# A two-block convolution kernel: programs written out by images, the first unit's planes formed on GpSimd, and the scale applied with the high and low parts

## The chip, the cores and the metric

The kernel runs on one core of a Trainium2 chip. The metric is the device time of one execution in microseconds. Engine names in the profile: PE is TensorE, DVE VectorE, ACT ScalarE, POOL GpSimd, SP SyncE.

## The reference

The input x is 4 images of 96 channels and 128 x 128 pixels, float32. Two residual blocks follow, each on a group normalisation (32 groups of 3 channels, no learned factors):

```
x = x + attention(gn(x))
x = x + conv_block(gn(x))

attention: layer norm over channels -> 1x1 convolutions to q (96), k (24), v (24)
           -> depthwise 3x3 -> attention over channels, 8 heads of 12 x 12,
              with l2-normed q and k and a temperature -> 1x1 projection
conv_block(y): cat(conv1x1(y), conv3x3(y), conv5x5(y), conv3x3 dilated by 2 (y)) -> 1x1 to 96
```

All four convolutions of the second block and the 1x1 behind them are linear, so the kernel folds them into one 5x5 convolution.

## The kernel before, in words

An image stays in SBUF as X (96 partitions x 16384). Per image there are these stages.

1. Projection (PE L712, in 32 tiles of 4 rows): ScalarE norms a tile (L915), PE projects it, ScalarE squares (L921), VectorE sums and scales (L1237, L1252), GpSimd adds a bias and stores it in another order (L596).
2. Depthwise 3x3 (PE L733 to L735, 24 chunks): VectorE builds band matrices (L1278), ScalarE evicts chunks (L947, L950) and sums the next image's rows.
3. Gram products of q and k (PE L761) on strips that VectorE copies (L1303), then a softmax chain of small steps, then attention (PE L796). VectorE adds the residual, which gives x1 in X, 2 x 512 columns at a time (L1364, 16 per image), and ScalarE sums squares of x1 (L1021). A group is averaged by a small product (`group_mean`, L693). Columns of `small` hold the statistics: MG the group mean, VG its variance, SA the scale, SBI the bias.
4. The 5x5 convolution, in 11 units of 12 rows (4 blocks of 3 rows; the last has fewer). It is a fast convolution: from normed rows (`y2`) differences in the row direction give five planes per block (`pln`, `planes`, L1408 to L1424), sums of neighbouring columns give `cs`, both are split into a high f16 part (`hi`, copied to `hi2`; ACT `highs`, L1052 to L1063) and a low one (`low`; DVE `lows`, L1474). DMAs place the low parts on other partitions beside the high ones (`place_first`, `place_groups`, `place_low`, SP and ACT queues), and PE multiplies with the weights in five groups (L865; L860 are products with low parts put off to the end of a group). VectorE combines the products (L1505, L1523), forms output rows (L1536), GpSimd adds the residual (L611) and SP writes out. For units 2 to 10 GpSimd makes two of the planes (L621).

Unit 0 has five blocks, the first being the rows at the image's edge, and goes in two parts: planes 3 and 4 first (part 0), planes 0 to 2 then (part 1), so that PE can begin early. Its first 7 rows are normed by ScalarE (L1039), the rest by VectorE (L1560).

Each engine runs a program of its own, and the order is written out by hand. Each of the five programs has an outer loop over the 4 images (`Fori(0, B)`), with counters in semaphores. While PE would idle between statistics, `keep_warm` (L688) gives it products of no use.

In the set-up, VectorE makes 32 bn_stats over image 0's rows (L1162) as they land, between steps on the weights. PE folds the convolutions to `folded` (L675), ScalarE copies them (L894). `split_weights` on GpSimd (L544 to L589) scales them by WSC, makes the fast convolution's weights and splits them into `wh` and `wl`; it runs in image 0, beside the depthwise stage. PE waits for its end (`s_split`) before the first group mean of the Gram stage, VectorE before the first column sums of unit 0.

## Time and profile before

| | us |
|---|---|
| median of 3 runs | 1769.56 |
| lowest and highest | 1764.85, 1773.46 |
| the profiled execution | 1766.19 |
| its span, first to last instruction | 1764.4 |

The profiled execution is one run; its span leaves out what lies before the first and after the last instruction. The mean granted clock of TensorE is 0.969 of full speed (2.4 GHz); the lower level, 1.2 GHz, reads 0.50 in a window. A line of the timeline gives start, duration, engine, source line, operation, output<-inputs, shapes, the count of like instructions merged, and in brackets the idle time before and what ended it.

### The profile page before, as it was taken

The page shows a single profiled execution, that of the slowest core. Times are in us where ns is not written, and L with a number is a line of the kernel's source. Part 1 is how long each engine was busy: PE and PEld are TensorE (multiplying, and loading weights), DVE is VectorE, ACT ScalarE, POOL GpSimd, SP SyncE. Part 2 cuts the span into 40 slices and gives each one's busy share as a digit, 9 for nine tenths or more (in the row PEclk, how much of TensorE's full clock was granted, in tenths as well). Part 3 has the DMA queues.
Part 4 walks back from the last instruction along what each step waited for, and adds up shares of the span by engine and source line. Part 5 has one row for each costly group of instructions (what it writes and reads, how often), then busy time and mean ns, then how long its engine had stood idle before and what let it go on. Part 6 is the DMA issues. An engine that isn't in the chain of part 4 may idle for free.

```text
span 1764.4 us, 40341 instructions
## 1 busy us (share of the span) xinstructions
PE 1674.1 (95%) x13429; PEld 1578.1 (89%) x13429; DVE 1502.6 (85%) x1950; ACT 1012.0 (57%) x1638; POOL 541.0 (31%) x351
## 2 busy tenths in 40 slices
PE   5989988999999999899999999999999999989998
PEld 5989857999989996899999997799999999689998
DVE  5788848999868877999978886899997887699996
ACT  2746656564366667656438566755636666664551
POOL 5799910223254000122328000032235500012222
PEclk9999978999999997999999999799999999899999
DMA  7012113566611210566650220266661021055453
GB/s 186 0 32 67 46 31 79 152 166 170 167 46 32 72 40 1 127 176 163 171 142 0 67 71 6 54 156 167 171 176 56 27 71 46 1 121 142 123 151 98
DMA packets 101196, 166.24 MB, mean 94 GB/s; under 512 B 40010, under 2 KB 74411, under 8 KB 100940
## 3 DMA queue, kind: packets, MB, share of 16 engines
q1 hardware_dynamic: 77932, 138.95, 31.1%
q10 hardware_dynamic: 23168, 26.04, 4.6%
q8 instruction: 55, 0.90, 0.2%
q14 instruction: 41, 0.34, 0.1%
HBM read 52.20 MB, written 25.17 MB: 44 GB/s over the span
## 4 chain that ended last, share of the span: by engine, by line
PE 50%; issue 17%; DVE 17%; POOL 9%; DMA 2%; ACT 2%; SPq 2%; DVEq 1%; POOLq 0%; ACTq 0%
PE ps L865 14%; PE ps L712 12%; PE ps L733 6%; PE ps L735 5%; PE ps L734 5%; PE ps L761 3%; PE ps L796 3%; DVE region L1474 3%; DVE region L1408 2%; DVE region L1505 2%; POOL region L611 2%; DVE region L1523 2%; POOL W L552 1%; POOL W L571 1%; DVE region L1536 1%
## 5 line engine op out<-in xcount | busy, mean ns | idle before, releaser
L865 PE MATMUL ps<-region,W 128*96 128x256 f16 (+4 forms) x7156 | 803.3, 272 | 15.6 <-DMA region<-region 15.6
L865 PEld LDWEIGHTS ps<-region,W 128*96 128x96 f16 (+2 forms) x7156 | 780.6, 122 | 31.4 <-issue 22.0
L621 POOL TENSOR_TENSOR region<-region 96x528 f32<-96x528 f32 (+1 forms) x72 | 96.4, 1343 | 924.9 <-DVE region L1474 923.6
L1278 DVE TENSOR_TENSOR region<-V,band 128x2322 f32<-128x2322 f32 (+2 forms) x104 | 260.8, 2518 | 59.9 <-PE ps L735 57.6
L1058 ACT ACTIVATE region<-region 96x1584 f16<-96x1584 f32 (+2 forms) x88 | 110.8, 1301 | 331.2 <-DVE region L1419 317.9
L733 PE MATMUL ps<-region 128*128 (+1 forms) x1152 | 229.1, 281 | 12.6 <-DVE region L1278 9.2
L735 PE MATMUL ps<-region 128*128 (+1 forms) x1152 | 223.7, 276 | 0.0
L734 PE MATMUL ps<-region 128*128 (+1 forms) x1152 | 223.4, 276 | 0.0
L712 PE MATMUL ps<-proj,region 96*128 96x240 f32 x1024 | 210.7, 369 | 8.3 <-DVE region L1536 8.3
L712 PEld LDWEIGHTS ps<-proj,region 96*128 96x128 f32 x1024 | 196.1, 192 | 22.0 <-issue 8.7
L1505 DVE SCALAR_TENSOR_TENSOR region<-ps,small,region 96x768 f32<-96x768 f32 (+1 forms) x220 | 203.7, 989 | 12.6 <-PE ps L865 11.3
L1474 DVE TENSOR_TENSOR region<-region 96x792 f16<-96x792 f32 (+10 forms) x176 | 197.5, 1180 | 5.0 <-ACT region L1058 4.8
L611 POOL TENSOR_TENSOR region<-region,X 96x1536 f32<-96x1536 f32 (+1 forms) x44 | 124.0, 2818 | 224.7 <-DVE region L1536 224.7
L733 PEld LDWEIGHTS ps<-region 128*128 128x128 f32 x1152 | 175.7, 193 | 17.9 <-issue 15.7
L596 POOL TENSOR_TENSOR region<-region,cbias 128x576 f32 (+1 forms) x124 | 175.8, 1418 | 46.7 <-DVE region L1252 43.2
L734 PEld LDWEIGHTS ps<-region 128*128 128x128 f32 x1152 | 176.0, 193 | 0.0
L735 PEld LDWEIGHTS ps<-region 128*128 128x128 f32 x1152 | 175.9, 193 | 0.0
L950 ACT ACTIVATE region<-ps 128x768 f32 (+1 forms) x80 | 65.8, 822 | 144.2 <-PE ps L735 144.2
L1052 ACT ACTIVATE region<-region 96x1584 f16<-96x1584 f16 (+2 forms) x88 | 113.9, 1295 | 0.3
L1252 DVE TENSOR_TENSOR region<-ps,region 128x576 f32<-128x576 f32 x124 | 94.0, 758 | 18.4 <-DVE region L1242 5.4
L915 ACT ACTIVATE region<-X,small 96x512 f32 (+1 forms) x128 | 101.6, 802 | 8.2 <-issue 7.4
L1536 DVE TENSOR_TENSOR region<-region 96x256 f32<-96x256 f32 (+3 forms) x176 | 88.4, 543 | 20.1 <-DMA out_dram<-region 18.4
(196 smaller groups left out, 2075.5 us busy)
## 6 DMA issues: line engine op xcount, KB each, us to landing
region<-region SPq DMA_DIRECT2D x116, 247.5 KB, 4.0
region<-in_x_dram SPq DMA_DIRECT2D x128, 192.0 KB, 2.4
out_dram<-region SPq DMA_DIRECT2D x40, 576.0 KB, 4.2
region<-region ACTq DMA_DIRECT2D x72, 247.5 KB, 2.5
X<-in_x_dram SPq DMA_DIRECT2D x30, 576.0 KB, 6.0
region<-region SPq DMA_DIRECT2D x36, 247.4 KB, 4.9
X<-in_x_dram SPq DMA_DIRECT2D x19, 384.0 KB, 11.3
region<-region SPq DMA_DIRECT2D x24, 185.6 KB, 3.5
```

The lines of the kernel that those rows point to most:

```text
L596: pool.tensor_tensor(Q[:, :, bass.ds(t * AR, AR)].rearrange("p c r -> p r c"), pq[:, i], cbias[:].unsqueeze(1).broadcast_to([P, AR, CO]), ...
L611: pool.tensor_tensor(ob[:, 0:r * W], ob[:, 0:r * W], X[:, bass.ds(u * UR * W, r * W)], ALU.add).then_inc(s_res, 1)
L712: last = mm(ps[:, 2 * i + r // 2, r % 2 * 256:r % 2 * 256 + NP], y1[:, i, r * W:(r + 1) * W], proj[:], start=True, stop=True)
L733: mm(o, T[:, i, 3 * c + 1, 0:W], src, start=True, stop=False)
L734: mm(o[:, 1:H], T[:, i, 3 * c, 0:W], src[:, 0:H - 1], start=False, stop=False)
L735: last = mm(o[:, 0:H - 1], T[:, i, 3 * c + 2, 0:W], src[:, 1:H], start=False, stop=True)
L865: last = mm(o, w, src, start=k == 0, stop=k == len(steps) - 1, skip_group_check=split and ck > 0)
L1052: act.activation(hi2[0:C, a:e, x:z], hi[0:C, a:e, x:z], ACT.Copy).then_inc(s_h, 1)
L1058: act.activation(dst[0:C, a:e, x:z], src, ACT.Copy).then_inc(s_h, 1)
L1278: v.tensor_tensor(T[:, i, 3 * c:3 * c + m].rearrange("p m (i j) -> p m i j", j=3), taps.broadcast_to([P, m, BW // 3, 3]), mask.broadcast_t ...
L1474: v.tensor_tensor(low[:, :, x:end], src, hi[0:C, a:e, x:end], ALU.subtract).then_inc(s_l, 1)
L1505: step = lambda dst, g, factor, src: v.scalar_tensor_tensor(row(dst), product(i, g, blocks), col(factor), row(src), ALU.mult, ALU.add).the ...
```

## The change

PE's and VectorE's loops over the images become Python loops, so that their programs hold four copies of an image's instructions, with waits on constants; the other three engines keep theirs. The scaling of the folded weights goes from GpSimd to ScalarE, behind the projection of image 0. PE no longer waits for `s_split` before the Gram stage. Six bn_stats go ahead of VectorE's wait for the weights. Unit 0's planes and wide column sums come from GpSimd, on x1 itself, and begin when two of x1's tiles are added: no scale is in them, and since they are differences the mean falls out, except for plane 4, to which VectorE adds the mean's share later, and the first block, which VectorE fills with x1 less the mean. `highs` and `lows` of unit 0 multiply by SA. Unit 0's buffers move. ScalarE's order in unit 0 puts the high part of part 1 before the copy of part 0; the first set's squares are taken in two halves; 22 warm-up products replace 40. VectorE's wait for `s_split` moves to the first low parts.

```diff
-        LOWF_AT, PLNF_AT, Y2F_AT = LOW_AT, Y2_AT - 5 * PLAIN, ACC_AT
-        YF = 5 * OR + 2
-        assert LOWF_AT + 5 * BLK // 2 <= PLNF_AT and Y2F_AT + YF * RW <= OB_AT + UR * W
+
+
+        LOWF_AT, PLNF_AT, CSF_AT, Y2F_AT = LOW_AT, Y2_AT - 5 * PLAIN, RING // 2 + 5 * BLK // 2, RING + 5 * BLK // 2
+        YF = OR + 2
+        assert LOWF_AT + 5 * BLK // 2 <= PLNF_AT and 5 * NPT * PC <= 5 * BLK // 2 and (YF + 5) * RW <= 5 * BLK // 2
...
-        N_SPLIT = 13 + NRT * 6 + 2
+        N_SPLIT = 12 + NRT * 6 + 2
...
-                pool.wait_ge(s_fold, N_COPIES + 5)
-                pool.wait_ge(s_dv, N_WSC)
-                plain = W32[:, FOLDED_AT:FOLDED_AT + 5 * 5 * C]
-                step(pool.tensor_scalar(plain, plain, col(WSC), None, ALU.mult))
+                pool.wait_ge(s_fold, N_COPIES + 6 + 5)
...
+                def first_planes():
+
+                    _, _, pln, yb, cs = buffers(0)
+                    rows = X[:, 0:(4 * OR + OR) * W].rearrange("p (r j c) -> p r c j", j=HC, c=2)
+                    taps = lambda t, c, count: rows[:, t + 1:t + 1 + 4 * OR, c] \
+                        .rearrange("p (k t) j -> p k t j", t=OR)[:, :, 0:count]
+                    slots = lambda x, end, c: pln[:, 1:5, x * RW:end * RW] \
+                        .rearrange("p k (t c j) -> p k t c j", c=2, j=PC)[:, :, :, c, 1:1 + HC]
+                    plane = lambda k, end, x: pln[:, k:end, x * RW:(x + 1) * RW]
+                    twice = f32at(Y2F_AT + YF * RW, 5 * RW).rearrange("p (k e) -> p k e", k=5)
+
+                    def done(n):
+                        pool.wait_ge(s_fp, b * NFP + n + START)
+
+                    def column_sums(k, end, x, y):
+                        pairs = pln[:, k:end, x * RW:y * RW].rearrange("p k (q e) -> p k q e", e=RW)
+                        dst = cs[0][:, k:end, 0:PC] if x == 3 else cs[1][:, k:end]
+                        pool.tensor_tensor(dst.rearrange("p k (q j) -> p k q j", j=PC), pairs[:, :, :, PC:RW],
+                                           pairs[:, :, :, 1:1 + PC], ALU.add).then_inc(s_fp, 1)
+
+                    def take(dst, a, d):
+                        pool.tensor_tensor(dst, a, d, ALU.subtract).then_inc(s_fp, 1)
+
+                    def point_0_and_inf(k, end, n):
+                        done(n)
+                        take(twice[:, k:end], plane(k, end, 1), plane(k, end, 0))
+                        take(plane(k, end, 2), plane(k, end, 2), plane(k, end, 1))
+                        done(n + 2)
+                        take(plane(k, end, 0), twice[:, k:end], plane(k, end, 0))
+                        take(plane(k, end, 2), plane(k, end, 2), plane(k, end, 1))
+                        done(n + 4)
+                    pool.wait_ge(s_x1, b * SETS * 2 + 2 + START)
+                    pool.wait_ge(s_o, (b * SETS + 2) * AR + START)
+                    for c in range(2):
+                        take(slots(3, 5, c), taps(2, c, 2), taps(1, c, 2))
+                    pool.memset(pln.rearrange("p k (q j) -> p (k q) j", j=PC)[:, :, 0:PC:PC - 1], 0.0).then_inc(s_fp, 1)
+                    pool.memset(yb, 0.0).then_inc(s_fp, 1)
+                    done(3)
+                    take(twice[:, 1:5], plane(1, 5, 4), plane(1, 5, 3))
+                    done(5)
+                    take(plane(1, 5, 3), twice[:, 1:5], plane(1, 5, 3))
+                    for n in (8, 10):
+                        for c in range(2):
+                            take(slots(4, 5, c)[:, :, 0], slots(4, 5, c)[:, :, 0], taps(1, c, 1)[:, :, 0])
+                        done(n)
+                    column_sums(1, 5, 3, 4)
+                    for c in range(2):
+                        take(slots(0, 3, c), taps(2, c, 3), taps(0, c, 3))
+                    point_0_and_inf(1, 5, 13)
+                    column_sums(1, 5, 0, 3)
+                    pool.wait_ge(s_pl0, b * NPL0 + 1 + START)
+                    own = yb.rearrange("p r e -> p (r e)")
+                    take(pln[:, 0, 0:3 * RW], own[:, 2 * RW:], own[:, 0:3 * RW])
+                    point_0_and_inf(0, 1, 19)
+                    column_sums(0, 1, 0, 3)
...
+                first_planes()
...
-            with pe.Fori(0, B) as b:
+            for b in range(B):
...
-                pe.wait_ge(s_split, N_SPLIT)
...
                 group_mean(st, VG, sv + N_VG2, 7)
-                keep_warm(0, 40)
+                keep_warm(0, 22)
...
-                                pe.wait_ge(s_h, n * NH + 4 + START)
+                                pe.wait_ge(s_h, n * NH + 5 + START)
...
+                with act.If(b < 1):
+                    act.wait_ge(s_dv, N_WSC)
+                    for k in range(5):
+                        act.activation(folded[:, k], folded[:, k], ACT.Copy, scale=col(WSC)).then_inc(s_fold, 1)
...
+                def squared_halves(k, n):
+
+                    for half in range(2):
+                        act.wait_ge(s_x1, (b * SETS + k) * 2 + half + 1 + START)
+                        squared(k, half, 2, n + half)
+                squared_halves(0, 0)
+                with act.Fori(1, SETS - 1) as k:
                     act.wait_ge(s_x1, (b * SETS + k + 1) * 2 + START)
-                    squared(k, 0, 1, k)
-                for half in range(2):
-                    act.wait_ge(s_x1, (b * SETS + SETS - 1) * 2 + half + 1 + START)
-                    squared(SETS - 1, half, 2, SETS - 1 + half)
+                    squared(k, 0, 1, k + 1)
+                squared_halves(SETS - 1, SETS)
...
-                        act.activation(dst[0:C, a:e, z:end], src, ACT.Copy).then_inc(s_h, 1)
+                        act.activation(dst[0:C, a:e, z:end], src, ACT.Copy, scale=1.0 if whole else col(SA)).then_inc(s_h, 1)
                     if whole == 0:
-                        for part in range(2):
-                            act.wait_ge(s_pl, n * NPL + (3, 7)[part] + START)
-                            plain(hi, part)
-                            act.wait_ge(s_pl, n * NPL + (4, 8)[part] + START)
-                            sums(hi, part)
-                            copied(part, 4 * part + 2)
-                            if part == 0:
-                                midway()
+                        act.wait_ge(s_pl0, b * NPL0 + 4 + START)
+                        plain(hi, 0)
+                        act.wait_ge(s_pl0, b * NPL0 + 6 + START)
+                        act.wait_ge(s_fp, b * NFP + 11 + START)
+                        sums(hi, 0)
+                        act.wait_ge(s_fp, b * NFP + 23 + START)
+                        plain(hi, 1)
+                        copied(0, 2)
+                        act.wait_ge(s_fp, b * NFP + 24 + START)
+                        sums(hi, 1)
+                        midway()
+                        copied(1, 6)
                     else:
-                        act.wait_ge(s_pl, n * NPL + 6 + START)
...
-                rows_normed(0, 0)
                 highs(0, 0, 0, lambda: rows_normed(1, 1))
...
+            statistics(0, 3)
             dve.wait_ge(s_w, NLOADS * 16)
...
-            statistics(0, 6)
+            statistics(3, 6)
...
-            with dve.Fori(0, B) as b:
+            for b in range(B):
...
-                yf, yn = buffers(0)[3], buffers(1)[3]
-                v.memset(yf[:, 0:2], 0.0)
-                for y in (yf[:, 2:], yn):
-                    v.memset(y.rearrange("p r (c j) -> p (r c) j", c=2)[:, :, 0:PC:PC - 1], 0.0)
+                _, _, pln0, yb, cs0 = buffers(0)
+                plane0 = lambda k, x, end: pln0[:, k, x * RW:end * RW]
+
+                def first_done(k):
+                    dve.wait_ge(s_pl0, b * NPL0 + k + START)
+
+                def first_block_rows():
+
+                    dve.wait_ge(s_fp, b * NFP + 4 + START)
+                    v.tensor_scalar(yb.rearrange("p r (c j) -> p r c j", c=2)[:, 2:, :, 1:1 + HC],
+                                    X[:, 0:OR * W].rearrange("p (r j c) -> p r c j", j=HC, c=2),
+                                    col(MG), None, ALU.subtract).then_inc(s_pl0, 1)
+                    first_done(1)
+                    own = yb.rearrange("p r e -> p (r e)")
+                    v.tensor_tensor(plane0(0, 3, 5), own[:, 2 * RW:4 * RW], own[:, RW:3 * RW], ALU.subtract).then_inc(s_pl0, 1)
+
+                def first_part():
+
+                    first_done(2)
+                    v.scalar_tensor_tensor(plane0(0, 3, 4), plane0(0, 3, 4), -2.0, plane0(0, 4, 5),
+                                           ALU.mult, ALU.add).then_inc(s_pl0, 1)
+
+                    dve.wait_ge(s_fp, b * NFP + 10 + START)
+                    one = pln0[:, 1:5, 4 * RW:5 * RW].rearrange("p k (c j) -> p k c j", c=2)[:, :, :, 1:1 + HC]
+                    v.tensor_scalar(one, one, col(MG), col(MG), ALU.add, ALU.add).then_inc(s_pl0, 1)
+
+                def first_sums():
+
+                    first_done(4)
+                    v.tensor_tensor(cs0[0][:, 0, 0:PC], plane0(0, 3, 4)[:, PC:RW], plane0(0, 3, 4)[:, 1:1 + PC],
+                                    ALU.add).then_inc(s_pl0, 1)
+                    one = pln0[:, :, 4 * RW:5 * RW]
+                    v.tensor_tensor(cs0[0][:, :, PC:2 * PC], one[:, :, PC:RW], one[:, :, 1:1 + PC], ALU.add).then_inc(s_pl0, 1)
+                yn = buffers(1)[3]
                 v.memset(col(MG), 0.0)
                 dve.wait_ge(s_x1, (b + 1) * 2 * SETS + START)
                 moments(st, tsums[:, 0:2 * SETS], MEAN2, MEAN)
                 assert st.n == N_MEAN2
+                v.memset(yn.rearrange("p r (c j) -> p (r c) j", c=2)[:, :, 0:PC:PC - 1], 0.0)
                 dve.wait_ge(s_pst, pst + 6 + START)
                 link(st, v.tensor_copy(col(MG), ps[0:C, 7, 0:1]))
                 link(st, v.tensor_tensor(col(DEV), col(MEAN2), col(MG), ALU.subtract))
                 link(st, v.tensor_tensor(col(VAR), col(SHIFT), col(SHIFT), ALU.mult))
                 link(st, v.scalar_tensor_tensor(col(VAR), col(DEV), col(DEV), col(VAR), ALU.mult, ALU.subtract))
-                dve.wait_ge(s_xs, (b + 1) * (SETS + 1) + START)
-                link(st, v.tensor_reduce(col(SQ), tsums[:, AT:], AX.X, ALU.add))
+                first_block_rows()
+                dve.wait_ge(s_xs, (b + 1) * (SETS + 2) + START)
+                link(st, v.tensor_reduce(col(SQ), tsums[:, 2 * SETS:], AX.X, ALU.add))
                 link(st, v.scalar_tensor_tensor(col(VG), col(SQ), 1.0 / (H * W), col(VAR), ALU.mult, ALU.add))
                 assert st.n == N_VG2
+                first_part()
                 dve.wait_ge(s_sqrt, b * 3 + 4 + START)
                 link(st, v.reciprocal(col(SA), col(RSTD)))
                 st.done(v.scalar_tensor_tensor(col(SBI), col(MG), -1.0, col(SA), ALU.mult, ALU.mult))
                 assert st.n == N_AFF2
+                first_sums()
...
+                        if whole == 0:
+                            v.scalar_tensor_tensor(low[:, :, x:end], src, col(SA), hi[0:C, a:e, x:end],
+                                                   ALU.mult, ALU.subtract).then_inc(s_l, 1)
+                            return
...
-                FIRST_ACT = 7
                 dve.wait_ge(s_st, sv + N_AFF2 + START)
-                v.tensor_scalar(yf[:, 2 + FIRST_ACT:].rearrange("p r (c j) -> p r c j", c=2)[:, :, :, 1:1 + HC],
-                                X[:, FIRST_ACT * W:(UR + OR) * W].rearrange("p (r j c) -> p r c j", j=HC, c=2),
-                                col(SA), col(SBI), ALU.mult, ALU.add).then_inc(s_y2v, 1)
-                planes(0, 0)
+                dve.wait_ge(s_split, N_SPLIT)
+                for part in range(2):
+                    lows(0, 0, 0, 0, part)
                 planes(1, 1)
                 lows(1, 1, 0, 1)
                 first_rows(0, 0, BPU)
```

## Rows read from the trace of the kernel before

**Rows 1.** The page: busy us of each engine, share of the span, instructions

```profile
PE 1674.1 (95%) x13429; PEld 1578.1 (89%) x13429; DVE 1502.6 (85%) x1950; ACT 1012.0 (57%) x1638; POOL 541.0 (31%) x351
```

**Rows 2.** The page: the chain that ended last, shares by engine

```profile
PE 50%; issue 17%; DVE 17%; POOL 9%; DMA 2%; ACT 2%; SPq 2%; DVEq 1%; POOLq 0%; ACTq 0%
```

**Rows 3.** Set-up: timeline of DVE and PE; landing of the first three row loads

```profile
31.37 10.77 DVE L1162 BATCH_NORM_STATS2 region<-X 96x6 f32<-96x512 f32 x18
...
39.20 0.48 PE L682 MATMUL ps<-small,region 96*96 96x5 f32 x2 [1.20 <-ACT region L895]
...
DMA to landing us min/median/max: 5.2/6.2/7.2
```

**Rows 4.** Depthwise stage of image 0: timeline, and a window (seventh value: granted clock)

```profile
105.98 8.36 POOL L544 TENSOR_SCALAR W<-W,small 96x2400 f32<-96x2400 f32 x1 [0.48 <-POOL region L596]
...
116.35 0.79 PE L733 MATMUL ps<-region 128*128 x2 [5.64 <-DVE region L1278]
...
114.00:122.00 8.00, 5.65 (x26) 5.66 (x27) 5.67 (x3) 0.00 (x0) 7.56 (x7) 0.59 0.09 25
```

**Rows 5.** Timeline of PE: start of the Gram products in images 0 and 1

```profile
226.48 0.48 PE L693 MATMUL ps<-small,gmean 96*96 96x1 f32 x2 [8.53 <-POOL W L589]
226.82 9.04 PE L761 MATMUL ps<-region 128*120 128x240 f16 x64
...
653.13 6.75 PE L761 MATMUL ps<-region 128*120 128x240 f16 x64
```

**Rows 6.** Timeline at the first, third (PE) and second (DVE) border between images

```profile
496.52 0.67 PE L712 MATMUL ps<-proj,region 96*128 96x240 f32 x2 [3.26 <-DVE region L1536]
...
1338.89 1.48 PE L712 MATMUL ps<-proj,region 96*128 96x240 f32 x6 [2.32 <-DVE region L1536]
...
920.13 0.15 DVE L1255 COPY small<-small 96x1 f32<-96x1 f32 x1 [1.97 <-issue]
```

**Rows 7.** Timeline of image 1 from the x1 tiles to unit 1

```profile
676.49 1.22 DVE L1364 SCALAR_TENSOR_TENSOR X<-ps,X 96x1024 f32 x1
...
692.51 0.08 DVE L1364 DVE_READ_ACCUMULATOR X<-ps,X  x1
...
697.08 1.21 ACT L1039 ACTIVATE region<-X,small 96x896 f32<-96x896 f32 x1 [0.42 <-DVE small L1387]
...
701.52 1.31 ACT L1058 ACTIVATE region<-region 96x1320 f16<-96x1320 f32 x1 [3.23 <-DVE region L1419]
...
705.18 0.65 SPq L365 DMA_DIRECT2D region<-region  x1
...
708.48 2.85 PE L865 MATMUL ps<-region,W 128*96 128x256 f16 x24 [1.69 <-DMA region<-region]
708.95 1.86 ACT L1058 ACTIVATE region<-region 96x1980 f16<-96x1980 f32 x1 [1.54 <-DVE region L1415]
...
714.36 1.25 DVE L1411 TENSOR_TENSOR region<-region 96x1056 f32<-96x1056 f32 x1 [0.19 <-DVE region L1474]
...
717.16 0.90 ACT L1098 ACTIVATE region<-ps,small 96x768 f32<-96x768 f32 x1 [2.62 <-PE ps L865]
...
719.84 2.51 ACT L1058 ACTIVATE region<-region 96x1584 f16<-96x1584 f32 x2 [1.78 <-DVE region L1415]
...
735.21 0.64 PE L860 MATMUL ps<-region,W 96*96 96x256 f16 x4 [1.29 <-DMA region<-region]
```

**Rows 8.** Timeline: DVE beside POOL, with one operand from PSUM and with none

```profile
215.03 0.59 POOL L568 TENSOR_TENSOR W<-W 96x192 f32<-96x192 f32 x1
215.04 0.59 DVE L1211 SCALAR_TENSOR_TENSOR small<-small 96x1 f32<-96x1 f32 x1
...
877.48 4.71 DVE L1505 SCALAR_TENSOR_TENSOR region<-ps,small,region 96x768 f32<-96x768 f32 x5
877.53 2.90 POOL L611 TENSOR_TENSOR region<-region,X 96x1536 f32<-96x1536 f32 x1 [14.67 <-DVE region L1536]
```

**Rows 9.** Groups of POOL by form, whole span (count, busy us, mean ns, idle before)

```profile
L621 POOL TENSOR_TENSOR region<-region 96x528 f32<-96x528 f32 x64 | 83.8, 1311 | 923.6 <-DVE region L1474 923.6
```

105 lines of the change are left out of this document (41 added, 64 removed).

## The prediction

> **What bounds the kernel now.** I read four views in this order: the busy shares, the chain of waits, the timeline around the places that the diff touches, and the windows with the granted clock. TensorE is busy 95% of the span and VectorE 85% [rows 1], and half of the chain that ended last is PE work [rows 2]. So a change pays only where PE stands still or runs slowly. The edited places that show this are four: the set-up; the first image's depthwise stage and the wait behind it; the three borders between images; and, four times, the passage from the last x1 tile to the second unit of the 5x5 stage.
>
> **The change part by part.** Gains are negative.
>
> *a. Set-up.* Six of the 24 statistics that VectorE makes before the weight maximum move ahead of the wait for the weights. Eighteen take 10.77 us, so six take 3.6 [rows 3]. The three loads that they read land 5.2 to 7.2 us after issues from 7.1 to 8.1, that is by 15.3, and VectorE would otherwise wait, so they fit before its set-up steps. But VectorE then comes to the maximum 3.6 us earlier, at about 38.5, and the product that it reads starts at 39.20 [rows 3]. It waits to about 39.8, which leaves some 2.2 of the 3.6. Ends: 0 (the steps behind are held) and -3.6. I take **-2.2**.
>
> *b. Depthwise stage of image 0.* GpSimd's scaling of the folded weights (L544) lasts 8.36 us; beside it VectorE's band matrix waits, and PE idles 5.64 us [rows 4]. The change gives that scaling to ScalarE as five instructions on 480 elements, at a time when ScalarE has finished its tiles and the first eviction is still ahead: nothing on the path. GpSimd's other splitting steps move up by as much and now meet the early bands, for which I keep 0.8 of the wait. After the gap the granted clock is 0.59 over 8 us, the lower level for most of it, which is 3.3 us of lost PE time [rows 4]. Sum -(5.64-0.8)-3.3 = **-8.1**. Ends: -4 (the splitting steps take the gap's place) and -9.
>
> *c. The wait for the split weights.* In image 0 PE stands 8.53 us in front of the group mean until GpSimd's last memset. Then its first 64 Gram products take 9.04 us, where image 1 takes 6.75: the clock again [rows 5]. The wait is deleted, and the rest (strips, sums) was there. VectorE and PE now do the strips and small statistics beside GpSimd's last steps; I put 1 us against it. -8.53-2.29+1.0 = **-9.8**. Ends: -6 and -10.8. What is late next is the weights' placing on SP, which follows the split; it moves up by b's 7 us or so and the first unit comes over 40 us later, so nothing waits.
>
> *d. Borders between images.* The PE and VectorE programs are written out, so their jump back is gone. PE's gap there is 3.26 us at the first border, 2.32 at the third, the second between them, together 8.2 [rows 6]. The row names VectorE's last outputs, but only PE's second tile needs what came last; VectorE itself idles 1.97 us after it with "issue" as the cause [rows 6], and both then start together: it is the jump. GpSimd, ScalarE and SP keep their loops, whose jumps lie in idle time. I take **-7.6**, keeping 0.2 per border. Ends: 0 (the new code is fetched just as late) and -8.2. The Trainium skill, Advanced Engine Details and Errata, Control Flow Timing, gives about 108 ns for a compare-and-branch; by that page's figure, an estimate, the three borders would give 0.3 us and the forecast would be 1737.
>
> *e. From x1 to the second unit, four times.* Times of image 1 [rows 7]. The scale is known at 697.08 (call it T). Then rows are scaled, planes formed, and only at 701.52 is the first high part made; the first low part is sent at 705.18, PE starts at 708.48, VectorE starts unit 1's planes at 714.36, ScalarE its high parts at 719.84, and PE gets the low parts that unit 1 needs at 735.21. With the change the planes exist at T. ScalarE's own work between 701.52 and 719.84 is the 18.3 us less its idle times of 1.54 and 1.78, and less some 0.4 of the 2.62 in which its queue issued three DMAs: 14.6 us. That chain now starts at T, if nothing else is late: unit 1's high parts start at T+14.7 instead of T+22.8, a gain of 8.
>
> T itself moves, and this is where I choose. GpSimd makes 24 instructions per image. From a two-input row of 192 elements (0.59 us) and one of 528 (1.311) [rows 8, 9] comes 0.18 us + 2.15 ns per element. Up to the wide column sums these are two of 512, six of 528, four of 256, one of 264, two of 768, one of 792 and two memsets: 2.6+7.9+2.9+0.8+3.7+1.9+0.8 = 20.6 us. They start when two tiles of x1 are added, at 676.5 [rows 7], so they end near 697.5. VectorE's statistics run from 692.6 to T [rows 7], so they meet GpSimd's last four or five. [Rows 8] show what that costs: a two-input VectorE instruction on a single column (L1211) took 0.59 us, starting and ending with GpSimd's L568. So each such step waits out the GpSimd instruction in flight, and they alternate. Placing the three two-input steps of the variance, the two of the first block's rows, the one of VG, and the one of SBI in this way, against GpSimd's 528, 528, 792, 396 and four of 132, T comes at about 702, 5 us later. Uncontended it would be 697. ScalarE's chain adds 0.3 for the first column sums. So unit 1's high parts start at 702+14.9 = 716.9, 2.9 us earlier. PE starts unit 0 at about 709 (low part sent at T+3.7, the same 3.3 to land), 0.5 later than now, but its second half (93 products at 0.11) finds its parts there. Everything behind 719.84 follows at the same distances, and PE, which would come to the low parts at 730.6, waits to 732.3. Gain 2.9 x 4 = **-11.6**. Ends per image: -7 (T stays; GpSimd's last planes still hold the copies by 1.3) and +2 (T at 707). The 18 fewer warm-up products leave PE idle for some 3 us before unit 0; if that lost the clock as b's gap did, 3.3 us would go, of which 1.7 lie in the wait before 732.3. That is inside the ends.
>
> The Trainium skill, SBUF — State Buffer, SBUF: two separate sides, says that a VectorE instruction in a two-port mode also takes the shared ports, with one input too. No row here shows it for one input. By the page the two added tensor_scalars would each wait out one more short GpSimd step, an estimated 1 us per image, and the forecast would be 1734.
>
> GpSimd's work during the adding of x1 costs VectorE nothing: those adds have one operand in PSUM, and the like instruction L1505 ran 4.71 us for five beside L611's 2.90, both their usual lengths [rows 8]. Register sums saved by constant waits, the moved memsets and the halved first square (0.3 us) I cost at nothing: they lie in the slack above.
>
> **Sum.** -2.2-8.1-9.8-7.6-11.6 = -39.3. The profiled execution took 1766.19 us around a span of 1764.4, so 1726.9 there. The median of the three runs is 1769.56, 3.4 above it; the forecast is for the median, 1730.
>
> **The rivals.** *No collision in the statistics (T stays).* For it: the steps are short and the order of GpSimd's list might just miss them. Against: L1211. Then e gives 7 x 4 = 28: 1714. *Only image 0 gains.* T moves to 705 or later and eats the rest of e, and the borders stay: a, b, c alone, -20: 1750. For it: the alternation could be worse than I placed it. *The x1 adds are blocked* (the one on the slower side). If each of GpSimd's instructions held up a VectorE add of x1, as L568 held L1211, the stage, which PE and VectorE share with no slack, would stretch by up to GpSimd's 20.6 us per image, 82 in all, without e's gain: 1769.6-27.7+82 = 1824. It decides against the change from about 7 us per image on. Against it: L1505 beside L611. *The written-out programs are read late*, at borders and elsewhere, and take back what the rest gives: within 0.5% of 1769.6. Against it: image 0, whose code also comes for the first time, shows no such gaps in its 5x5 stage. That PE's deleted wait is implied by another would be seen as the gap staying; the group mean's inputs are ready before, so I give it no chance of its own.
>
> **How the numbers follow.** Forecast case 0.62, no collision 0.15, image 0 alone 0.13, code read late 0.05, x1 blocked 0.05. A measurement here can tell 0.5%, 8.8 us. The first three are faster (0.90), the fourth the same (0.05), the last slower (0.05). The unknown costs move the likeliest case from 1714 to 1748; the range takes in both neighbours, 1710 to 1752, and leaves out the last two and some edges.
>
> **What would show it.** In image 0: no gap of PE before L733 around 110, none before the group mean, the Gram products near 6.75 us. At the borders: PE gaps under 0.5 us. In each image: two-input statistics steps of VectorE longer than 0.3 us beside GpSimd, T 4 to 6 us later, and 14 to 15 us from T to unit 1's high parts. Wrong would be: x1 adds (1.22 us now) longer, borders with 2 us or more, or T unmoved.

## The result and the profile after

The changed kernel takes 1724.91 us (median; 1724.12 to 1725.26), the kernel before 1768.41 in the same comparison: a ratio of 0.9751, 95% interval 0.9726 to 0.9776. That is 43.5 us less; the forecast was 39.3 less and 1730, so the time lies in the range. The profiled execution took 1725.26 around a span of 1723.0, 41.4 under the span before. The lines move: PE's projection is now L772, the depthwise products L793 to L795, the Gram products L821, the group mean L753, the keep-warm products L748, attention L855, the 5x5 products L924 and L919; VectorE's band matrices are L1346, its x1 additions L1432, unit 0's low parts L1554; ScalarE's high parts L1122; GpSimd's first planes L632.

The page of the changed kernel, parts 3 (the instruction queues: packets, MB, share of the DMA engines) and 4 (the chain, shares by engine):

```profile
q8 instruction: 47, 0.77, 0.2%
q14 instruction: 34, 0.28, 0.1%
...
PE 70%; DVE 12%; issue 11%; ACT 3%; POOL 1%; SPq 1%; DMA 1%; DVEq 1%; ACTq 0%; POOLq 0%
```

PE now has 70% of the chain where it had 50, "issue" 11 where it had 17, GpSimd 1 where it had 9 [rows 2]. What PE still waits for, longest first:

```profile
PE ps L753 <- DVE small L1483: 19.5, 4, 5.0
...
PE ps L924 <- DMA region<-region: 5.7, 4, 1.8
PE ps L793 <- DVE region L1355: 4.4, 6, 0.9
```

The wait of 8.53 us for GpSimd's memset and the 5.64 us in the depthwise stage [rows 4, 5] are gone. A new one stands on top: PE's second group mean behind the x1 stage waits 4.9 us an image for the variance (L1483). It is not PE's loss by itself, since unit 0's data isn't there; it shows that VectorE's statistics got slower.

Set-up, first border and third border, on PE's timeline (start, duration, engine, line, operation, count, idle time before):

```profile
39.22 0.48 PE L742 MATMUL ps<-small,region 96*96 96x5 f32 x2 [1.20 <-ACT region L954]
...
47.00 1.41 PE L772 MATMUL ps<-proj,region 96*128 96x240 f32 x3
...
469.69 1.89 PE L772 MATMUL ps<-proj,region 96*128 96x240 f32 x8
...
1298.99 1.28 PE L772 MATMUL ps<-proj,region 96*128 96x240 f32 x5
```

The projection starts 2.24 us earlier than at 49.24, and there is no bracket at a border: PE goes from one image to the next without idle time, where it had 3.26, 2.67 and 2.32 us.

The passage to unit 0 of image 1, VectorE, then GpSimd, ScalarE and PE. x1 ends with the first row, at 664.99:

```profile
663.77 1.22 DVE L1432 SCALAR_TENSOR_TENSOR X<-ps,X 96x1024 f32 x1
...
665.23 0.21 DVE L1271 TENSOR_SCALAR small<-small 96x1 f32<-96x1 f32 x1
...
666.42 1.19 DVE L1478 TENSOR_TENSOR small<-small 96x1 f32<-96x1 f32 x1
667.64 1.23 DVE L1479 SCALAR_TENSOR_TENSOR small<-small 96x1 f32<-96x1 f32 x1
668.90 0.61 DVE L1445 TENSOR_SCALAR region<-X,small 96x384 f32<-96x384 f32 x1
669.55 1.54 DVE L1450 TENSOR_TENSOR region<-region 96x264 f32<-96x264 f32 x1
...
671.20 0.79 DVE L1483 SCALAR_TENSOR_TENSOR small<-small 96x1 f32<-96x1 f32 x1
...
673.04 0.21 DVE L1488 SCALAR_TENSOR_TENSOR small<-small 96x1 f32<-96x1 f32 x1
```

```profile
663.64 5.21 POOL L632 TENSOR_TENSOR region<-region 96x528 f32<-96x528 f32 x4
668.93 1.87 POOL L628 TENSOR_TENSOR region<-region 96x792 f32<-96x792 f32 x1
670.76 3.79 POOL L632 TENSOR_TENSOR region<-region 96x396 f32<-96x396 f32 x5
```

```profile
673.38 1.40 ACT L1122 ACTIVATE region<-region,small 96x1320 f16<-96x1320 f32 x1 [0.56 <-DVE small L1488]
...
687.71 2.51 ACT L1122 ACTIVATE region<-region 96x1584 f16<-96x1584 f32 x2 [1.53 <-DVE region L1515]
```

```profile
680.78 2.83 PE L924 MATMUL ps<-region,W 128*96 128x256 f16 x24 [0.77 <-DMA region<-region]
```

The granted clock there (columns: stretch, length, busy time and count of PE, PEld, DVE, ACT and POOL, granted clock, DMA share, GB/s):

```profile
678.00:681.00 3.00, 2.23 (x20) 2.07 (x20) 2.42 (x2) 3.00 (x4) 0.00 (x0) 1.00 0.64 142
```

The reader should see four things. The two-input steps on a single column took 1.19, 1.23 and 0.79 us beside GpSimd's 528- and 396-element instructions, and L1488 took 0.21, because the instruction that it met had only 0.20 us to go. The one-tensor step L1271 took 0.21 beside them. ScalarE starts with the scale (T) at 673.38, 8.4 us after x1's end, where it had been 4.5 [rows 7]. And unit 1's high parts start at T + 14.3, 22.7 us after x1's end, where it had been 27.2. Image 1 is the mildest of the four: in images 0, 2 and 3 the first single-column step, L1477, is held too (1.23 us), L1479 takes 1.9 beside the 792-element instruction, T comes 9.2 us after x1's end, and unit 1's high parts start 23.5 to 23.6 us after it. From image 0, VectorE and GpSimd:

```profile
251.52 1.23 DVE L1477 TENSOR_TENSOR small<-small 96x1 f32<-96x1 f32 x1
...
254.05 1.90 DVE L1479 SCALAR_TENSOR_TENSOR small<-small 96x1 f32<-96x1 f32 x1
```

```profile
251.43 2.57 POOL L632 TENSOR_TENSOR region<-region 96x528 f32<-96x528 f32 x2
254.08 1.86 POOL L628 TENSOR_TENSOR region<-region 96x792 f32<-96x792 f32 x1
```

### The profile page after: what moved, and what is told of

Its sections match the earlier page's. It is cut to its first block, busy times and chain, and to the rows that moved or that the text cites. A ratio compares the mean times of both kernels' runs of the same rounds, so it can differ in the third digit from the quotient of the medians.

```text
span 1723.0 us, 39391 instructions
## 1 busy us (share of the span) xinstructions
PE 1645.8 (96%) x13285; PEld 1550.5 (90%) x13285; DVE 1492.8 (87%) x1930; ACT 1011.6 (59%) x1647; POOL 637.2 (37%) x446
## 4 chain that ended last, share of the span: by engine, by line
PE 70%; DVE 12%; issue 11%; ACT 3%; POOL 1%; SPq 1%; DMA 1%; DVEq 1%; ACTq 0%; POOLq 0%
PE ps L924 28%; PE ps L772 12%; PE ps L793 8%; PE ps L795 7%; PE ps L794 7%; PE ps L821 3%; PE ps L855 3%; DVE region L1557 1%; DVE region L1587 1%; DVE region L1508 1%; POOL region L670 1%; PE ps L735 1%; DVE region L1605 1%; PE ps L919 1%; DMA region<-region 1%
## 5 line engine op out<-in xcount | busy, mean ns | idle before, releaser
L924 PE MATMUL ps<-region,W 128*96 128x256 f16 (+4 forms) x7156 | 796.7, 270 | 5.7 <-DMA region<-region 5.7
L924 PEld LDWEIGHTS ps<-region,W 128*96 128x96 f16 (+2 forms) x7156 | 774.9, 122 | 20.6 <-issue 14.1
L1346 DVE TENSOR_TENSOR region<-V,band 128x2322 f32<-128x2322 f32 (+2 forms) x104 | 257.7, 2488 | 59.2 <-PE ps L795 56.1
L1122 ACT ACTIVATE region<-region 96x1584 f16<-96x1584 f32 (+1 forms) x80 | 98.1, 1273 | 311.0 <-DVE region L1519 306.2
L793 PE MATMUL ps<-region 128*128 (+1 forms) x1152 | 228.2, 280 | 10.0 <-DVE region L1355 4.4
L795 PE MATMUL ps<-region 128*128 (+1 forms) x1152 | 222.8, 275 | 0.0
L772 PE MATMUL ps<-proj,region 96*128 96x240 f32 x1024 | 210.1, 368 | 0.5 <-DVE region L1605 0.4
L772 PEld LDWEIGHTS ps<-proj,region 96*128 96x128 f32 x1024 | 195.2, 191 | 14.4 <-issue 1.2
L793 PEld LDWEIGHTS ps<-region 128*128 128x128 f32 x1152 | 174.6, 192 | 16.5 <-issue 14.8
L1557 DVE TENSOR_TENSOR region<-region 96x792 f16<-96x792 f32 (+6 forms) x160 | 175.1, 1153 | 0.9 <-DMA region<-region 0.8
L795 PEld LDWEIGHTS ps<-region 128*128 128x128 f32 x1152 | 174.9, 192 | 0.0
L632 POOL TENSOR_TENSOR region<-X 96x512 f32<-96x512 f32 (+1 forms) x16 | 29.2, 1844 | 385.3 <-PE ps L855 385.3
```

Of the source, the lines that this page charges most:

```text
L772: last = mm(ps[:, 2 * i + r // 2, r % 2 * 256:r % 2 * 256 + NP], y1[:, i, r * W:(r + 1) * W], proj[:], start=True, stop=True)
L793: mm(o, T[:, i, 3 * c + 1, 0:W], src, start=True, stop=False)
L795: last = mm(o[:, 0:H - 1], T[:, i, 3 * c + 2, 0:W], src[:, 1:H], start=False, stop=True)
L924: last = mm(o, w, src, start=k == 0, stop=k == len(steps) - 1, skip_group_check=split and ck > 0)
L1346: v.tensor_tensor(T[:, i, 3 * c:3 * c + m].rearrange("p m (i j) -> p m i j", j=3), taps.broadcast_to([P, m, BW // 3, 3]), mask.broadcast_t ...
L1557: v.tensor_tensor(low[:, :, x:end], src, hi[0:C, a:e, x:end], ALU.subtract).then_inc(s_l, 1)
```

## The experiments

All are timed against the kernel before; differences below are from the changed kernel's 1724.9 unless another is named. The runs of one version spread by 1 to 3 us, with a loop back on PE by 5; a difference of 2 us can be told where the runs don't overlap, smaller ones only with the trace. Durations of the projection end, and those of the depthwise stage begin, at the first L795 product, 0.5 us after the first L793.

### The loops

```diff
-            for b in range(B):           # PE
+            with pe.Fori(0, B) as b:
-            for b in range(B):           # VectorE
+            with dve.Fori(0, B) as b:
```

Both loops put back:

> The changed kernel with the loops over the images put back on TensorE and VectorE. Theory (the jump back costs): PE gaps of 2.3 to 3.3 us at the three borders between images, VectorE idle about 2 us there with issue as the cause, 1724.9 + 8.5 = about 1733. Rival (writing out is worth nothing, the border was VectorE's last outputs): 1725, with the same start of the projection as in the changed kernel.

Measured: 1744.88 (ratio to before 0.9865, 0.9833 to 0.9897), 20.0 slower, more than twice what the kernel before had shown at its borders. PE's idle times there were 4.65, 4.59 and 4.14 us. So each loop was tried alone, and the written-out programs alone in the kernel before.

> The changed kernel with the loop over images put back on TensorE alone; VectorE's program stays written out. With both loops back the kernel ran 20 us longer than the changed one (1744.9 against 1724.9), with 4.65, 4.59 and 4.14 us of idle TensorE at the three borders, where the kernel before had 3.26, 2.67 and 2.32, and two first projections at half clock. Theory: the idle time is TensorE's own jump back, during which it reads instructions, and VectorE's jump (2.1 us) lies beside it; then the same gaps of 4.1 to 4.7 us stand here and the time is 1744, within 2. Rival 1: the border was the sum of two jumps one after the other, TensorE's first matmul of an image waiting for VectorE's first instruction too; then the gaps are 2.3 to 2.6 us, the clock is not lost, and the time is 1733. Rival 2: what costs is VectorE's loop alone; then it is 1726.

Measured: 1742.66 (0.9855, 0.9826 to 0.9884). From its trace, PE's timeline at the first border, the granted clock behind it (columns as above), and the instruction queues:

```profile
473.62 1.96 PE L772 MATMUL ps<-proj,region 96*128 96x240 f32 x4 [4.50 <-issue]
```

```profile
473.00:480.00 7.00, 6.38 (x18) 5.52 (x19) 0.55 (x1) 1.48 (x3) 0.82 (x1) 0.55 0.41 115
```

```profile
q8 instruction: 55, 0.90, 0.2%
q14 instruction: 34, 0.28, 0.1%
```

The theory holds: the idle time is PE's own, since VectorE's program is written out here. The gaps, 4.50, 4.62 and 4.32, are 13.4 us; behind them PE starts at the lower clock level (0.55 over 7 us here, 0.71 and 0.54 behind the other two), and the three projections take 59.8, 59.0 and 60.4 us against 57.8, 57.0 and 57.3, 7.1 more. Of the 20.5 the depthwise stages give back 1.5 (1.1 of it in image 3) and the 5x5 stages 1.6. With PE's loop, queue q8 carries 55 packets, 0.90 MB, without it 47; one of them lies in the gap. The Trainium skill, Runtime: NRT & Kernel Launch, Instruction fetch mechanics, says that a branch to code outside the window held on chip makes the engine fetch it before it goes on; the packets agree.

> The changed kernel with the loop over images put back on VectorE alone. TensorE's alone cost 17.8 us (1742.7 against 1724.9), both 20. Theory: VectorE's jump back takes 2.1 us at a border, and TensorE, whose program is written out, has the next image's first projection before it, so that the jump shows only in what TensorE waits for there: 1725 to 1728. Rival: the two are substitutes, each stopping the border by itself, and this costs as much as TensorE's alone: 1740.

Measured: 1729.35 (0.9765, 0.9750 to 0.9780), 4.4 slower and past the top of what was expected. VectorE idles at each border as expected:

```profile
DVE small L1323 <- issue: 6.0, 3, 2.0
```

PE has no gap, but its projections of images 1 to 3 take 58.5, 57.7 and 58.3 us, 2.3 more in all, and 5x5 units start 0.1 to 1.1 us later after x1's end. The rival that this loop alone costs as much as PE's is out.

> The kernel before with one part of the change alone: both loops over images written out. If the borders are worth what they showed in the kernel before (3.26 + 2.67 + 2.32 = 8.25 us idle, and 1.6 us for the first border's projection at a lower clock), the time is 1768.4 - 9.9 = 1758.5. If they are worth 20 us, as putting them back into the changed kernel cost, it is 1748.5. Theory: 1758.5, since the longer gaps and the lost clock came only with the loops in the changed kernel. If the written-out program cost anything in instruction reading, it would be 1760 or more.

Measured: 1757.49 (0.9936, 0.9916 to 0.9956), 11.0 faster than before in that comparison, within 1.0 of the theory and far from 20. PE's gaps are gone there too (projections begin at 492.97, 910.88 and 1328.95 with none), and q8 has 48 packets. So the borders were worth what the kernel before showed. The clock's part does not stand out: the projection behind the first border is 1.6 us shorter, those behind the other two 0.3 and 0.9 longer.

Why the same jump costs 4.5 us in the changed kernel and 2.3 to 3.3 in the old one can be followed one step further, with the packets on queue q8. Before each of PE's first products the last such packet ends 2.0 to 2.2 us earlier, in both kernels; what differs is when it ends (us from the start of PE's idle time):

| border | packet starts | packet ends | first product after its end | idle |
|---|---|---|---|---|
| kernel before, 1 | 0.09 | 1.13 | 2.14 | 3.26 |
| 2 | -0.55 | 0.66 | 2.02 | 2.67 |
| 3 | -0.65 | 0.27 | 2.04 | 2.32 |
| PE's loop back, 1 | 0.94 | 2.35 | 2.15 | 4.50 |
| 2 | 0.38 | 2.66 | 1.97 | 4.62 |
| 3 | 0.76 | 2.25 | 2.07 | 4.32 |

In the kernel before, the packet ahead of this one starts 4.8 us before the idle time; in the changed kernel 0.2 to 0.5 us before it, so that the two follow each other closely. So the longer gap goes with a later packet. Why the packet is later was not tested and stays open.

### The wait for the split weights

```diff
+                pe.wait_ge(s_split, N_SPLIT)
                 pe.wait_ge(s_ns, (b + 1) * AT + START)
                 group_mean(st, MEANX, sv + N_MEANN, 3)
```

> The changed kernel with TensorE's wait for the split weights put back before the Gram stage. Theory: in image 0 TensorE stands from 210.8 us to the end of GpSimd's splitting near 219, then runs the Gram products at the lower clock: +8.3 +2.3 +0.9, about 1736. Rival (what TensorE waits for anyway implies it): 1725.

Measured: 1734.31 (0.9796, 0.9767 to 0.9826), 9.4 slower. PE's waits in image 0, 200 to 260 us:

```profile
PE ps L753 <- POOL W L592: 7.9, 1, 7.9
```

The rest is the Gram stage after it, 21.11 us from its start to attention against 19.67. The theory holds in its mechanism, at less than its price: the idle time is 7.9 and not 8.3, the clock's share 1.4 and not 2.3, and the 0.9 of the x1 stage does not come back (19.8 us here as in the changed kernel).

### The scaling of the folded weights

```diff
-        act.activation(folded[:, k], folded[:, k], ACT.Copy, scale=col(WSC))     # 5 times, ScalarE
...
+        step(pool.tensor_scalar(plain, plain, col(WSC), None, ALU.mult))         # once, GpSimd
```

> The changed kernel with the scaling of the folded weights back as one step of 8.4 us on GpSimd, in place of the five scaled copies on ScalarE. Theory: GpSimd's later steps (the split weights, then its share of the taps) come 8.4 us later, TensorE waits 5.6 us in image 0's depthwise stage as it did before and works some us at half clock, and the stage is back at 112 us: 1725 + 5.6 to 8.1 = 1730.5 to 1733. Rival: in the changed kernel the split weights are no longer waited for ahead of the Gram stage, so that part of the delay is absorbed: below 1727.

Measured: 1729.35 (0.9776, 0.9750 to 0.9802), 4.4 slower: the mechanism, at less than its expected price.

```profile
104.16 7.25 POOL L550 TENSOR_SCALAR W<-W,small 96x2400 f32<-96x2400 f32 x1 [0.48 <-POOL region L602]
```

```profile
112.19 0.79 PE L796 MATMUL ps<-region 128*128 x2 [5.14 <-DVE region L1345]
```

PE idles 5.14 us for the band matrix, then runs at the lower level (granted clock 0.50 from 112 to 116); the depthwise stage takes 110.0 us, where the changed kernel takes 105.5 and the kernel before, without its wait for the weights, 111.2. The difference from the expectation is in what the changed kernel has in the gap's place: 4.4 us in six waits for L1355 and 1.2 for an eviction, where before there were 2.9 and none.

### The statistics of the set-up

```diff
-            statistics(0, 3)
             dve.wait_ge(s_w, NLOADS * 16)
...
-            statistics(3, 6)
+            statistics(0, 6)
```

> The changed kernel with the six statistics steps of the set-up in one block where they were, in place of three ahead and three behind. Theory: the projection starts 2.2 us later, at 49.2 in place of 47.0, and all behind it with it: 1724.9 + 2.2 = 1727. Rival: the first projection waits for a transfer or the weights just as long, and the time is 1725.

Measured: 1726.98 (0.9753, 0.9740 to 0.9766), 2.1 slower, as expected, and no run of the one overlaps one of the other. The projection starts at 49.57, not 47.00. In the other ten versions of the changed kernel, which leave the set-up as it is, it starts at 46.65 to 47.95, so the 2.2 is good to about 1 us in a single trace.

### GpSimd's head start

```diff
-                    pool.wait_ge(s_x1, b * SETS * 2 + 2 + START)
+                    pool.wait_ge(s_x1, (b + 1) * SETS * 2 + START)
```

> The changed kernel, with GpSimd's first planes held until the whole of x1 is added, not from its second step on. GpSimd works on them for 26.1 us without a break (649.15 to 675.23 for image 1), 15.8 us of that ahead of x1's end. Theory: the head start is what pays; started at x1's end the planes of points 3 and 4 are there 10 us later, and unit 0 starts some 2 us later than now, but its third group needs the other planes, done at x1's end + 26 us and then rounded and copied for some 6 us, and TensorE stands still for 10 us or so there; 12 us for each image, so 1725 + 48 = 1773 (1755 to 1785), about as slow as the kernel before. Rival: the planes have slack enough behind the statistics, and the head start is worth less than 3 us an image: under 1737.

Measured: 1786.68 (ratio to before 1.0100, 1.0072 to 1.0127): 61.8 slower than the changed kernel, and slower than the kernel before. The direction holds; the price is 15.4 us an image and not 12, and it lies in another place than expected. The first waits of PE and of ScalarE:

```profile
PE ps L924 <- ACT region L1117: 67.9, 4, 17.3
```

```profile
ACT region L1122 <- POOL region L632: 43.1, 4, 10.8
```

Unit 0 starts 30.8 us after x1's end, 14 to 15 later than now and not 2. ScalarE's order has the high part of planes 0 to 2 ahead of the copies that part 0 needs, so a wait for the last of GpSimd's planes holds up the first half as well. The expectation followed the data and forgot the queue. In the changed kernel these planes come in time, with 0.9 us to spare: ScalarE reads them from 675.42 on, and their last subtraction ended at 674.55.

### The collisions on VectorE

Five steps on single columns were rewritten so that only one operand is a tensor and the other a per-partition scalar:

```diff
-        v.tensor_tensor(col(VAR), col(SHIFT), col(SHIFT), ALU.mult)
+        v.tensor_scalar(col(VAR), col(SHIFT), col(SHIFT), None, ALU.mult)
-        v.scalar_tensor_tensor(col(VAR), col(DEV), col(DEV), col(VAR), ALU.mult, ALU.subtract)
+        v.tensor_scalar(col(VAR), col(DEV), col(DEV), col(VAR), ALU.mult, ALU.subtract)
```

> The changed kernel with the five two-input single-column steps of VectorE between the end of x1 and the scale written as tensor_scalar with one tensor input and columns as scalars; same arithmetic. Theory (two-input steps wait out GpSimd's instruction in flight): these steps fall from 0.8 to 1.2 us to 0.15 to 0.25, the scale is known some 2 us earlier per image, but GpSimd's last planes hold the high part of part 1, so 1.5 us per image is left: 1724.9 - 6 = about 1719. Rival (the steps are slow for a reason of VectorE's own, or for a semaphore): same durations, 1725.

Measured: 1720.11 (1719.28 to 1720.94; ratio to before 0.9719, 0.9689 to 0.9748), 4.8 faster than the changed kernel. These are the groups of the changed kernel and then of this version (busy us and mean ns of 4):

```profile
L1479 DVE SCALAR_TENSOR_TENSOR small<-small 96x1 f32<-96x1 f32 x4 | 6.9, 1735 | 0.1
...
L1478 DVE TENSOR_TENSOR small<-small 96x1 f32<-96x1 f32 x4 | 4.9, 1221 | 0.1
L1477 DVE TENSOR_TENSOR small<-small 96x1 f32<-96x1 f32 x4 | 3.9, 964 | 0.1
L1483 DVE SCALAR_TENSOR_TENSOR small<-small 96x1 f32<-96x1 f32 x4 | 3.1, 786 | 0.1
L1450 DVE TENSOR_TENSOR region<-region 96x264 f32<-96x264 f32 x4 | 2.8, 708 | 0.1
L1460 DVE TENSOR_SCALAR region<-region,small 96x512 f32<-96x512 f32 x4 | 2.8, 688 | 0.0
...
L1455 DVE SCALAR_TENSOR_TENSOR region<-region 96x132 f32<-96x132 f32 x4 | 1.2, 293 | 0.1
```

```profile
L1455 DVE SCALAR_TENSOR_TENSOR region<-region 96x132 f32<-96x132 f32 x4 | 6.1, 1528 | 0.1
L1450 DVE TENSOR_TENSOR region<-region 96x264 f32<-96x264 f32 x4 | 5.3, 1318 | 0.1
...
L1460 DVE TENSOR_SCALAR region<-region,small 96x512 f32<-96x512 f32 x4 | 5.0, 1244 | 0.0
...
L1479 DVE TENSOR_SCALAR small<-small 96x1 f32<-96x1 f32 x4 | 1.1, 268 | 0.1
L1478 DVE TENSOR_SCALAR small<-small 96x1 f32<-96x1 f32 x4 | 0.8, 210 | 0.1
L1488 DVE TENSOR_SCALAR small<-small 96x1 f32<-96x1 f32 x4 | 0.8, 210 | 0.1
L1483 DVE TENSOR_SCALAR small<-small 96x1 f32<-96x1 f32 x4 | 0.8, 210 | 0.1
L1477 DVE TENSOR_SCALAR small<-small 96x1 f32<-96x1 f32 x4 | 0.8, 209 | 0.1
```

A step on the same column with the same arithmetic took 1.22 us with two tensor operands and 0.21 with one, in the same place beside the same GpSimd work. That two tensors are not slow by themselves is seen in image 1 of the changed kernel, where L1477 began 0.06 us ahead of GpSimd's instruction and took 0.16. The collision is shown. But only a third of it is won: the five steps got shorter by 15.4 us over the four images, and L1450, L1455 and L1460, which now met GpSimd's 528-, 792- and 396-element instructions, longer by 9.6. Unit 0 starts 15.3 us after x1's end in each image, where the changed kernel had 15.8 to 16.8.

One step further, the 264-element step (L1450) moved behind the variance:

> As one_input, and VectorE's 264-element difference of the first block (1.54 us in the changed kernel, with GpSimd beside it) comes after the group variance instead of before. Theory: the scale is known about 5 us after the end of x1 instead of 8.3; GpSimd's last planes are then the wait that is left; 1.8 us per image, 1718. Rival: 1725; or, if GpSimd's planes are not in the way, 3.3 us per image, 1712.

Measured: 1722.40 (0.9727, 0.9697 to 0.9756), so not faster; a miss. Unit 0 again started 15.3 us after x1's end, and it ran slower. PE in image 1, the one-tensor version and then this one:

```profile
668.01 7.34 PE L748 MATMUL ps<-ident 128*128 128x128 f32 x44
678.45 4.43 PE L924 MATMUL ps<-region,W 128*96 128x256 f16 x24 [3.10 <-DMA region<-region]
```

```profile
667.36 6.97 PE L748 MATMUL ps<-ident 128*128 128x128 f32 x44
679.04 5.33 PE L924 MATMUL ps<-region,W 128*96 128x256 f16 x24 [4.71 <-DMA region<-region]
```

The 22 keep-warm products (44 matmuls in the trace, two for each) begin when the variance is known. Known earlier, they end earlier, PE stands idle for 4.7 us, and its first 24 products take 5.33 us against 2.83 in the changed kernel. The length of the idle time alone does not settle this: in image 0 of the one-tensor version PE idled 2.7 us and the 24 products took 2.83, in image 2 of the kernel before it idled 2.0 and they took 4.50. Filling the idle time was tested by more products:

```diff
-                keep_warm(0, 22)
+                keep_warm(0, 48)      # 53 in the reordered version
```

> The version with the single-column statistics steps in one-tensor form, and 48 in place of 22 matmuls behind the second group mean that keep TensorE busy until unit 0's data is there. Without the further ones TensorE stood idle up to 3.4 us ahead of unit 0 and did its first 24 matmuls of image 1 in 4.43 us at a granted clock of 0.70; the 5x5 stage took 203.8 us in images 1 and 2 and 202.8 to 203.0 in images 0 and 3. Theory: the clock is lost in that idle time; with it filled the stage takes 202.8 us in each image, so 1720.1 - 2 = 1718, and the time from x1's end to unit 0 stays at 15.3 us. Rival: the added matmuls run past the data's arrival and delay unit 0 by up to 1 us an image: 1721 or more.

> The one-tensor version with the 264-element step behind the second group mean's input (1722.4 us, 1718 had been expected), now with 53 in place of 22 keep-warm matmuls. In that version the group mean came 1.1 us earlier after x1's end, so its 22 keep-warm matmuls ended earlier too, TensorE waited 4.7 us for unit 0's copy and ran the first 6 us of the unit at a granted clock of 0.50 to 0.53; the 5x5 stage took 203.5 to 205.0 us. Theory: the miss was this clock alone, since unit 0 itself started no earlier (15.3 us after x1's end in both); filled, it is the same as the other version, 1718 within 1. Rival: the reorder costs something of its own, and it stays above 1720.

Measured: 1725.81 (0.9746, 0.9732 to 0.9759) and 1723.77 (0.9738, 0.9724 to 0.9751): both slower than without. PE of the first, image 1:

```profile
669.92 12.56 PE L748 MATMUL ps<-ident 128*128 128x128 f32 x96
682.31 2.82 PE L924 MATMUL ps<-region,W 128*96 128x256 f16 x24
```

The 1718 was missed in both; the theory's mechanism is there, and the rival's outweighs it. The clock loss is gone (2.82 us for the 24 products, the 5x5 stage 202.1 us in images 0 to 2 and not 202.7 to 203.8), and the added products ran past the data by 2 to 3 us, where the rival had said up to 1: unit 0 came 17.3 to 18.6 us after x1's end. The products had been sized at 0.11 us each, which is the time of one matmul of the trace at full clock; a product is two of them and the first ones run at the lower level. A count in between, by an estimate from these rows some 34 to 37, should keep both gains; it was not tried. The one-tensor version is the fastest that was run.

## Why the prediction was right, and where it was not

Term by term, in spans of the profiled executions, and what putting one part back costs:

| term | forecast | in the trace | put back |
|---|---|---|---|
| a, set-up | -2.2 | -2.2 | 2.1 |
| b, depthwise stage of image 0 | -8.1 | -5.6 | 4.4 |
| c, wait for split weights | -9.8 | -11.3 | 9.4 |
| d, borders | -7.6 | -8.7 | 20.0; alone in the old kernel 11.0 |
| e, x1's end to the end of the 5x5 stage, four images | -11.6 | -14.5 | not separable |
| other stages | 0 | +1.0 | |
| sum (of the unrounded terms) | -39.3 | -41.4 | |

**a** held: VectorE was stopped at the product L742 and waited 1.16 us for it, which left 2.2 of the 3.6.

**b** was too large by 2.5. The 5.64 us gap and the low clock behind it did go, but "I keep 0.8 of the wait" failed. VectorE's L1355 and an eviction are late instead, 5.6 us in seven waits where there had been 2.9.

**c** was too small by 1.5. The 1 us put against it for VectorE's work beside GpSimd was not needed; PE goes from the depthwise stage to the Gram products without a gap. The group mean and the softmax were shorter as well, by 0.5 together. b and c together are -16.9, against the -17.9 forecast; that the two errors nearly cancel is luck. The x1 stage of image 0 also went from 20.7 us to 19.8, but that is not the wait's: with the wait put back, and in the old kernel with only its programs written out, it takes 19.8 too. In the profiled execution of the kernel before, PE ran at the lower clock level from 249 to 252 us, where that stage begins.

**d** held in size (0.2 us kept per border was not needed; the gaps are 8.25 of it, the projections behind them 0.5), and its cause is now shown, PE's own jump. The figure of 108 ns for a compare-and-branch from the Trainium skill (Advanced Engine Details and Errata, Control Flow Timing), and with it 1737, is out for this loop: a jump back cost PE 2.3 to 4.7 us and VectorE 2.0.

**e** was too small by 2.9. The chain behind T is as worked out, T + 14.3 where 14.9 was said. T moved by 3.9 us in image 1 and by 4.7 in the others, where 5 was said. The mechanism was right, single-column steps waiting out GpSimd's instructions, but of the list of seven only four were held in each image: in image 1 L1477, L1455 and L1488 took 0.16, 0.29 and 0.21 us, in the others L1450, L1455 and L1488 took 0.43, 0.29 and 0.21. Unit 0 starts 0.1 us earlier after x1's end in image 1 and 0.7 to 0.9 later in the others, on average the 0.5 later that was forecast, and at full clock (in image 1 granted clock 1.00 from 678 to 681); the keep-warm products, which wait for the variance, end only 0.8 to 1.8 us before it. So the gain is all in the shorter 5x5 stage, 203.0 to 203.4 us against 207.5 to 207.8 in images 0 to 2. The x1 additions are unchanged at 1.22 us, so the rival on the slower side is out. So is the Trainium skill's rule (SBUF — State Buffer, SBUF: two separate sides) in the form in which I had applied it: L1445 took 0.61 us in every version, also where it began 0.14 us into a 1.31 us GpSimd instruction (the version without the head start). For the other added step the rule agrees: L1460, one tensor operand of 512 elements, ended 0.28 or 0.29 us after the GpSimd instruction that it met, in the changed kernel, where it took 0.69 us, as in the one-tensor version, where it took 1.24.

**Other stages** were taken as unchanged. The largest part is image 3's depthwise stage, 99.1 us against 97.9, longer by up to 0.25 us in nine of ten equal stretches. The kernel before with only its programs written out shows the same 99.1, and so does the changed kernel with VectorE's loop back; with PE's loop back it is 98.0. So it goes with PE's written-out program. Why it is the last image alone is open. Image 0's projection is 0.7 longer, and the 0.9 less of its x1 stage stands against these.

The "put back" costs and the trace differ: a to d give 36 us put back and 28 in the trace, because the border costs more in the changed kernel than it did in the old. A part's price depends on which kernel it is tried in.

## What to carry to other kernels

A loop's jump back on an engine that is never idle is paid in full, and in the changed kernel again in the clock behind it. Look for it at the border as idle time: the trace calls its cause "issue" in one kernel and names another engine in the other, so the test is to write the loop out on that engine. When work is given to GpSimd beside VectorE's small statistics, write those with one tensor operand and scalars from columns, and expect the collision to move to the next two-tensor step. Keep-warm products must be counted from when they start to when the data comes; a change that starts them earlier ends them earlier, and in both trials here the surplus cost more (5.7 and 1.4 us) than the clock that it kept.

## What was not expected of the hardware

- The same jump back of PE's loop cost 2.3 to 3.3 us in one kernel and 4.1 to 4.7 in another, and in the second the projections behind the borders ran 2 to 3 us longer at a lower clock. In both, PE's first product comes 2.0 to 2.2 us after the end of a packet on q8, in the six borders of the table; in the second the packet ends later.
- PE's program is read on queue q8 and VectorE's on q14: PE's loop alone raised q8 from 47 packets to 55, and VectorE's alone raised q14 from 34 to 42.
- After idle times of 3.1 and 4.7 us, PE's next 24 products took 4.43 and 5.33 us; after 0.8 us, 2.83. But they also took 2.83 after 2.7 us, and 4.50 after 2.0 us in the kernel before.
- A two-tensor step of VectorE on one element per partition lasted up to 1.9 us beside GpSimd (L1479 in the changed kernel, L1488 in the version without the head start), nine times the 0.21 us of L1488 in the changed kernel.
- A one-tensor step of 384 elements was not held by GpSimd in any version, one of 512 elements (L1460) was held in every version.
